# Two gate stages and two routing stages: four more row buffers, one row tile in four normalised on ScalarE, and low one-hots built on GpSimd

## The reference, cut to what matters

```python
x = _layernorm(x + attention(x))                      # layer 0; layer 1 has a wavelet part here
gate = softmax(flat_x @ w_gate.T, axis=-1)            # [4096, 8]
topk_scores, topk_idx = top_k(gate, 2)
# layer 0: out = sum over the two experts of score * expert(x)
# layer 1: counts = bincount(a_e); keep = counts <= cap (1.25 * N / E = 640)
#          pos = place of the token in its expert's queue; experts over cap give nothing
x = _layernorm(x + experts(x))
```

## Time and profile before

| what | value |
|---|---|
| median of three runs | 1922.46 us |
| profiled execution, of which span | 1918.8 us, 1917.0 us |
| gate 0, route 0 up to the first low one-hot, map of route 0 | 19.1, 20.6, 27.5 us |
| gate 1, route 1 up to the first low one-hot, map of route 1 | 19.5, 19.7, 22.8 us |
| VectorE busy in these six stretches | 13.9, 17.4, 26.9, 14.0, 16.4, 22.1 us |
| TensorE busy in them | 14.9, 0.6, 20.9, 15.6, 0.6, 17.5 us |
| ScalarE busy in them | 8.3, 1.7, 0.0, 8.4, 1.7, 0.0 us |
| GpSimd busy in them | 0.4, 1.2, 0.0, 0.5, 2.5, 0.0 us |
| granted TensorE clock in them | 0.88, 0.56, 0.89, 0.84, 0.59, 0.90 |
| share of the DMA engines in them | 0.67, 0.93, 0.49, 0.66, 0.94, 0.15 |

### The profile page before, as it was taken

How to read it: one execution, slowest core, us unless ns; L and a number is a source line. 1 busy time by engine, 2 the same in 40 slices (tenths; PEclk the granted TensorE clock), 3 DMA queues, 4 the chain that set the end, 5 groups by cost and what they waited for, 6 DMA issues and landing times. The chain is left out here.

```text
span 1917.0 us, 38671 instructions
## 1 busy us (share of the span) xinstructions
PE 1690.9 (88%) x11908; PEld 1094.2 (57%) x11909; DVE 1142.3 (60%) x2436; ACT 893.3 (47%) x1523; POOL 394.9 (21%) x559
## 2 busy tenths in 40 slices
PE   8999999999999999998489999999999399934771
PEld 4523434344434444436379999999999357923551
DVE  5688898989898999858821111111111487887224
ACT  4437777677677776771023333333333252230233
POOL 2310000000010000040023333333333100001782
PEclk9979999999999999999789999999999699977896
DMA  6501222212222221426735666665666200034545
GB/s 212 183 24 49 57 57 58 56 56 56 59 57 59 55 59 56 129 55 185 258 113 168 186 169 187 171 184 169 186 168 186 94 1 1 1 131 136 71 53 176
DMA packets 118378, 207.52 MB, mean 108 GB/s; under 512 B 22064, under 2 KB 88176, under 8 KB 108848
## 3 DMA queue, kind: packets, MB, share of 16 engines
q1 hardware_dynamic: 89280, 171.29, 28.1%
q0 software_dynamic: 20352, 22.92, 7.4%
q10 hardware_dynamic: 8688, 12.58, 1.9%
HBM read 163.65 MB, written 56.10 MB: 115 GB/s over the span
## 5 line engine op out<-in xcount | busy, mean ns | idle before, releaser
L607 DVE TENSOR_REDUCE unit_max<-ps_ring 128x1 f32<-128x512 f32 x1024 | 640.3, 684 | 76.8 <-PE ps_ring L500 70.5
L593 ACT ACTIVATE w<-ps_scores 128x1024 f32<-128x1024 f32 x512 | 498.1, 1022 | 237.5 <-PE ps_scores L562 237.4
L500 PE MATMUL ps_ring<-k_stack,q_stack 96*128 96x512 bf16 x1024 | 359.2, 392 | 10.6 <-POOL v_padded L458 7.9
L562 PE MATMUL ps_scores<-q_stack,k_stack 98*128 98x512 bf16 x1024 | 306.4, 381 | 2.6 <-ACT w L593 2.5
L1475 PEld LDWEIGHTS m_ps_h<-m_xt,w1s 128*128 128x128 f32 x2272 | 267.2, 193 | 4.6 <-issue 0.9
L1475 PE MATMUL m_ps_h<-m_xt,w1s 128*128 128x128 f32 x2272 | 267.6, 276 | 0.6 <-issue 0.6
L1485 PE MATMUL m_ps_y<-w,m_ht 128*128 x1136 | 260.8, 383 | 0.0
L522 PE MATMUL ps_o<-w,v_padded 128*32 128x256 f32 x4096 | 260.6, 383 | 0.0
L500 PEld LDWEIGHTS ps_ring<-k_stack,q_stack 96*128 96x128 bf16 x1024 | 98.6, 96 | 253.7 <-DVE unit_max L607 181.4
L1485 PEld LDWEIGHTS m_ps_y<-w,m_ht 128*128 128x128 f32 x1136 | 210.1, 190 | 29.5 <-issue 0.2
L1507 ACT ACTIVATE m_ht<-m_ps_h,w1s 128x128 f32<-128x128 f32 x568 | 162.4, 368 | 97.0 <-PE m_ps_h L1475 97.0
(11 more groups left out here) (258 smaller groups left out, 1540.9 us busy)
## 6 DMA issues: line engine op xcount, KB each, us to landing
w1s<-in_w SPq DMA_DIRECT2D x71, 1028.0 KB, 4.9
o_raw<-o_transposed SPq DMA_DIRECT2D x64, 128.0 KB
rows<-g_rows SPq DMA_DIRECT2D x16, 512.0 KB, 4.6
y<-sums SPq DMA_DIRECT2D x16, 512.0 KB, 6.5
q_parts<-qk_part SPq DMA_DIRECT2D x16, 384.0 KB, 2.8
k_parts<-qk_part SPq DMA_DIRECT2D x16, 384.0 KB, 2.8
q_stack<-q_parts SPq DMA_DIRECT2D x64, 96.0 KB
k_stack<-k_parts SPq DMA_DIRECT2D x64, 96.0 KB
```

The costliest lines, as they stand in the source:

```text
L500: nc.tensor.matmul(out[:, :], qs[0:STACK, u, qt * P:(qt + 1) * P], ks[0:STACK, u, half * HALF:(half + 1) * HALF], start=True, stop=True).t ...
L562: mm = nc.tensor.matmul(p_s[kt % 2][:, half * HALF:(half + 1) * HALF], ks[:, u, kt * P:(kt + 1) * P], qs[:, u, half * HALF:(half + 1) * HALF],
L593: nc.scalar.activation(pt[:, kt, :], p_s[kt % 2][:, :], ACT.Exp, scale=SCALE)\
L607: nc.vector.tensor_reduce(unit_max[:, u % 2, half, qt:qt + 1], src[:, :], axis=AX.X, op=ALU.max).then_inc(ring_used, count)
```

## The change

**Gates.** The row buffers become eight, so no half waits for a buffer. VectorE normalises three tiles of each half, and ScalarE the fourth (`OWN = HB - 1`), with one activation each; a new semaphore `act_ready` tells SyncE and TensorE of it. VectorE's list keeps its order.

**Routes.** The constant `unit` and the copies into `value` go: GpSimd writes the token numbers into `value` directly (two iotas), and the maxima of the softmax are written into `value` too. The mask is written as bf16 by its addition. The eight scans become one scan over 256 elements in expert-major order, whose `resets` (0 at each expert's first tile) begin it anew; totals are stored expert-major, and the order of the additions to the slot numbers changes. Slot, hi and lo are computed for both choices at once on 512 and 64 elements.

**Map.** GpSimd builds the low one-hots, one 128x128 `tensor_scalar` with `is_equal` and a scalar per partition for each product, into four buffers of a batch each. In route 1 (`tiles` is 35) the last of the eight batches stays with VectorE as one 128x1024 instruction. The loops are written out instead of being rolled.

```diff
-    HB, HALVES, BUFS, TURNS = TB // 2, 2 * B, 4, 6
+    HB, HALVES, BUFS, TURNS = TB // 2, 2 * B, 8, 6
+        act_ready = mem.sem("g_act_ready")
+        OWN = HB - 1
...
                 for h in range(HALVES):
                     sp.wait_ge(ready, h + 1)
+                    sp.wait_ge(act_ready, h + 1)
                     sp.dma_start(halves[h], st[h % BUFS][:, :, :]).then_inc(stored[h % BUFS], 16)
...
-                    for t in range(HB):
+                    for t in range(OWN):
                         last = normalised(nc, c, st[h % BUFS][:, t, :], h * HB + t)
                     last.then_inc(ready, 1)
...
+                                if k == 0 and t == OWN:
+                                    pe.wait_ge(act_ready, 2 * b + h + 1)
...
             def _(act):
+                def norm(h):
+                    wait_from(act, turned, (h - BUFS) * 2 + 2)
+                    wait_from(act, stored[h % BUFS], h // BUFS * 16)
+                    for t in range(OWN, HB):
+                        i = h * HB + t
+                        last = nc.scalar.activation(st[h % BUFS][:, t, :], c.y[:, i, :], ACT.Identity,
+                                                    scale=c.rstd[:, i:i + 1], bias=c.nmr[:, i:i + 1])
+                    last.then_inc(act_ready, 1)
...
+        LOS, LO_BUFS = 2 * NT // DEEP, 4
+        on_pool = LOS if tiles > P // 2 else LOS - 1
+
+        def low_onehots(m):
+            for k in range(2):
+                for j in range(DEEP // 2):
+                    i = m * (DEEP // 2) + j
+                    last = nc.gpsimd.tensor_scalar(oh_lo[m % LO_BUFS][:, k, j, :], iota_p[:, :], lo[:, k, i:i + 1], None,
+                                             ALU.is_equal)
+            return last
...
+                for k in range(2):
+                    nc.gpsimd.iota(value[:, k, :, 0], pattern=[[P, NT]], base=-N, channel_multiplier=1, **imprecise)\
+                        .then_inc(made, 1)
+                nc.gpsimd.memset(resets[:, :, :], 1.0).then_inc(made, 1)
...
+                pool.wait_ge(lo_ready, 1)
+                for m in range(on_pool):
+                    if m >= LO_BUFS:
+                        pool.wait_ge(mapped, (m - LO_BUFS + 1) * DEEP)
+                    low_onehots(m).then_inc(lo_made, 1)
...
-                link(v.tensor_tensor(t["mask"][:, :, :], t["oh1"][:, :, :], t["oh2"][:, :, :], ALU.add))
-                v.tensor_copy(maskb[:, :], t["mask"][:, :, :].rearrange("p i e -> p (i e)")).then_inc(mask_done, 1)
+                v.tensor_tensor(maskb[:, :].rearrange("p (i e) -> p i e", e=E), oh1, oh2, ALU.add).then_inc(mask_done, 1)
...
-                for e in range(E):
-                    scan = v.tensor_tensor_scan(out=t["incl"][:, :, e], data0=unit[:, :], data1=totals[:, :, e],
-                                                initial=0.0, op0=ALU.mult, op1=ALU.add)
-                    link(scan)
+                link(v.tensor_copy(totals[:, :, :], p_n[:, 0:G].rearrange("p (i e) -> p e i", e=E)))
+                link(v.tensor_tensor_scan(out=incl[:, :, :].rearrange("p e i -> p (e i)"),
+                                          data0=resets[:, :, :].rearrange("p e i -> p (e i)"),
+                                          data1=totals[:, :, :].rearrange("p e i -> p (e i)"),
+                                          initial=0.0, op0=ALU.mult, op1=ALU.add))
...
-                for k, onehot in enumerate((t["oh1"], t["oh2"])):
-                    link(v.tensor_tensor(t["prod"][:, :, :], t["pos"][:, :, :], onehot[:, :, :], ALU.mult))
-                    link(v.tensor_reduce(small["slot"][:, :], t["prod"][:, :, :], axis=AX.X, op=ALU.add))
...
+                link(v.tensor_tensor(prod[:, :, :, :], oh12[:, :, :, :],
+                                     bcast(t["pos"][:, :, :].unsqueeze(1), [P, 2, NT, E]), ALU.mult))
+                link(v.tensor_reduce(slot[:, :, :], prod[:, :, :, :], axis=AX.X, op=ALU.add))
...
+                v.scalar_tensor_tensor(out=lo[:, :, :], in0=hi[:, :, :], scalar=-float(P), in1=slot[:, :, :],
+                                       op0=ALU.mult, op1=ALU.add).then_inc(lo_ready, 1)
...
-                for k, gain in enumerate((small["w1"], small["w2"])):
-                    link(v.tensor_copy(value[:, k, :, 0], token[:, :]))
-                    link(v.tensor_copy(value[:, k, :, 1], gain[:, :]))
...
+                for m in range(LOS):
+                    if m >= on_pool:
+                        dve.wait_ge(mapped, (m - LO_BUFS + 1) * DEEP)
+                        shape, i0 = [P, 2, DEEP // 2, P], m * (DEEP // 2)
+                        v.tensor_tensor(oh_lo[m % LO_BUFS][:, :, :, :],
+                                        bcast(iota_p[:, :].unsqueeze(1).unsqueeze(1), shape),
+                                        bcast(lo[:, :, i0:i0 + DEEP // 2].unsqueeze(3), shape),
+                                        ALU.is_equal).then_inc(lo_last, 1)
+                    for at in range(DEEP):
+                        i, k, u = m * (DEEP // 2) + at // 2, at % 2, m % 2 * DEEP + at
+                        wait_from(dve, mapped, m * DEEP + at - 2 * DEEP + 1)
...
+                for m in range(LOS):
+                    if m < on_pool:
+                        pe.wait_ge(lo_made, m + 1)
+                    else:
+                        pe.wait_ge(lo_last, m - on_pool + 1)
```

More of the change, by code:

```diff
@@ L857, in keep @@
                         .then_inc(logits_done, 1)
+                for h in range(4):
+                    norm(h)
                 for b in range(B):
-                    norm(2 * b)
-                    norm(2 * b + 1)
+                    copy(b)
                     if b > 0:
-                        copy(b - 1)
-                    if b > 1:
-                        keep(b - 2)
-                copy(B - 1)
-                keep(B - 2)
+                        keep(b - 1)
+                    if b < 2:
+                        norm(2 * b + 4)
+                        norm(2 * b + 5)
                 keep(B - 1)
@@ L966, in stage_route @@
         ones = mem.sb("e_ones", [P, P], BF16)
-        totals = mem.sb("e_totals", [P, NT, E])
-        unit = mem.sb("e_unit", [P, NT])
+        totals = mem.sb("e_totals", [P, E, NT])
+        incl = mem.sb("e_incl", [P, E, NT])
+        resets = mem.sb("e_resets", [P, E, NT])
+        prod = mem.sb("e_prod", [P, 2, NT, E])
+        oh12 = mem.sb("e_oh", [P, 2, NT, E])
+        slot = mem.sb("e_slot", [P, 2, NT])
         iota_e = mem.sb("e_iota_e", [P, E])
@@ L985, in stage_route @@
         ownf = mem.sb("e_ownf", [P, owners])
-        oh_lo = [mem.sb(f"e_oh_lo{h}", [P, 2, DEEP // 2, P]) for h in range(2)]
+        LOS, LO_BUFS = 2 * NT // DEEP, 4
+        oh_lo = [mem.sb(f"e_oh_lo{h}", [P, 2, DEEP // 2, P]) for h in range(LO_BUFS)]
         COLS = max(P, 2 * tiles)
@@ L1065, in _ @@
                 link(v.tensor_tensor(t["pr"][:, :, :], t["ex"][:, :, :], wide(small["rc"]), ALU.mult))
-                dve.wait_ge(made, 7)
-                link(v.tensor_reduce(small["w1"][:, :], t["pr"][:, :, :], axis=AX.X, op=ALU.max))
-                first_of(t["pr"][:, :, :], small["w1"], t["oh1"])
-                link(v.scalar_tensor_tensor(out=t["pr2"][:, :, :], in0=t["oh1"][:, :, :], scalar=-2.0,
+                gains, oh1, oh2 = [value[:, k, :, 1] for k in range(2)], oh12[:, 0, :, :], oh12[:, 1, :, :]
@@ L1071, in _ @@
+                dve.wait_ge(made, 10)
+                link(v.tensor_reduce(gains[0], t["pr"][:, :, :], axis=AX.X, op=ALU.max))
+                first_of(t["pr"][:, :, :], gains[0], oh1)
+                link(v.scalar_tensor_tensor(out=t["pr2"][:, :, :], in0=oh1, scalar=-2.0,
                                             in1=t["pr"][:, :, :], op0=ALU.mult, op1=ALU.add))
-                link(v.tensor_reduce(small["w2"][:, :], t["pr2"][:, :, :], axis=AX.X, op=ALU.max))
-                first_of(t["pr2"][:, :, :], small["w2"], t["oh2"])
@@ L1087, in _ @@
+                v.tensor_tensor(totals[:, :, :], incl[:, :, :], totals[:, :, :], ALU.subtract)
+                count = incl[:, :, NT - 1]
                 if fixed is None:
@@ L1141, in outer_products @@
                         v.scalar_tensor_tensor(
                             out=oh_hi[u], in0=bcast(iota_t[:, :].unsqueeze(1), [P, 2, tiles]),
-                            scalar=hi[:, k, bass.ds(i, 1)],
-                            in1=bcast(value[:, k, bass.ds(i, 1), :].rearrange("p i a -> p (i a)").unsqueeze(2),
-                                      [P, 2, tiles]),
+                            scalar=hi[:, k, i:i + 1],
+                            in1=bcast(value[:, k, i, :].unsqueeze(2), [P, 2, tiles]),
@@ L1162, in _ @@
                     pe.wait_ge(padded, len(hi_flat))
-                def outer_products(g, first, last):
-                    for u in range(2 * DEEP):
-                        pe.wait_ge(hi_done, g * (2 * DEEP) + u + 1)
```

(12 more changed lines are left out.)

64 lines of the change are left out of this document (28 added, 36 removed).

## The result

The changed kernel is slower. Four runs gave a median of 1938.76 us (1938.31 to 1943.49), four runs of the kernel before on the same chip 1922.39 us (1920.78 to 1922.85): 1.0102 of before, 95% interval 1.0088 to 1.0116. I had forecast 1909 us, in a range of 1903 to 1922 us.

A forecast was written before the change was run, and what follows sets the result against it. VectorE was taken to lead in the gates, routes and maps, which don't overlap. Gates -2.7, routes -2.4 and -2.6, maps -4.7 and -1.0 sum to -13.4 us: 1922.5 to 1909 us; 8-in-10 range 1903 to 1922.

The forecast's parts named there:

- P: Maps: time from one GpSimd low one-hot to the next; taken as 0.30 us, with waits for VectorE 0.35 and 0.33.
- The upper bound: Maps: at a two-input addition's rate, 2.1 ns per element, plus 0.043, a GpSimd one-hot of 128 elements takes 0.46 us.
- 120 P - 54.3: Whole kernel: change in time in us with P, GpSimd's time per low one-hot, left open.
- The meetings: Maps: each VectorE high one-hot keeps GpSimd out for 0.17 or 0.09 us, adding 0.05 and 0.03 us to P.
- the fast rival: Maps: GpSimd fast and hidden, P 0.32 in route 0, TensorE bounding route 1; -19.4 us, 1903 us; chance 0.17.
- The slower rival: Maps: VectorE and GpSimd exclude each other for whole instructions, 0.58 and 0.50 us per pair; +10.8 us, 1933 us; chance 0.14.
- The routes up to lo: Routes from their start to lo, clears included: -2.4 us in route 0 and -2.6 us in route 1.
- The scan: Routes up to lo: one scan of 256 elements takes 0.70 us, replacing eight that took 2.05; -1.35 us with gaps.
- the joint slots: Routes up to lo: slot, hi and lo for both choices together take 2.44 us instead of 3.57; -1.13 us.
- The strided read: Routes up to lo: strided reads of the totals cost nothing, or 0.5 us if they ran at half rate.
- The clears: GpSimd clears five more semaphores ahead of route 0, 0.06 us each; three more before the experts' first load, 0.2 per route.
- The gates: Gate stages: -1.6 us in gate 0 and -1.1 in gate 1, in all -2.7 us (bounds -1.4 and -3.5).

The follow-up runs named there:

- the split: Changed kernel with GpSimd making only every other low batch, four of eight in route 0 and three in route 1, VectorE the others; 1909.61 us, 0.9952 of before.
- the changed kernel with the row in PSUM: Changed kernel whose high one-hots read their row of tile numbers from PSUM, copied there by ScalarE; 1938.78 us, 1.01 of before; repeated, 1937.03 us.
- the gates alone: Kernel before the change with only the new gate stage; 1919.32 us, 0.9994 of before.

## Why the prediction was wrong

- **The step that failed** is the term for P in the maps: "I take 0.30, near the copy and the select, since the one-hot reads one tensor; 0.02 is for the scalar per partition." The one-hot took 0.60 us, 0.58 from one to the next without meetings. Two parts of it were off. The difference between `tensor_scalar` and a plain cast, 0.043 us, was read on 8 elements and added to a copy of 128; it grows with the elements, and at 128 it is 0.53 - 0.29 = 0.24 us with an immediate. The scalar per partition adds 0.07, not 0.02. The upper bound had the same 0.043 on top of the two-input rate and was added up wrongly: 0.2 + 128 x 2.1 ns + 0.043 is 0.51, not 0.46. It would have been no bound at 0.51 either: I took one input to be cheaper than two, but the one-input `tensor_scalar` costs 2.6 ns per element and the two-input addition of the earlier trace rows 2.1. By the formula, 120 P - 54.3, the measured 40.11 + 34.08 us give +19.9 us; the stages of the table show +22.3.
- **The Trainium skill**, GPSIMD Engine Reference, section Elementwise — side-by-side cycle accounting, gives at best about 1.8 cycles per element. I drew an estimate of 0.41 for P from it and set it aside because of a cast in the earlier trace rows. The one-hot's 2.6 ns per element lie above the page's best case, 769 ns for 512 elements or 1.5 ns each; the cast was the wrong witness for arithmetic.
- **The meetings** were right in kind. A high one-hot of VectorE was held for up to 0.15 us by a one-hot of GpSimd (the longest took 0.52 us for the 0.37 before; 24 in 8.98 us are 0.374 each, against 0.277), the hold that the fast rival used. VectorE's batch of 1024 elements held GpSimd for 1.68 - 0.60 = 1.08 us, and 1024 x 1.04 ns are 1.07: the hold is as long as the elements stream. I had counted 0.5 for it, against my own rule. In sum the meetings moved P by 0.04 and 0.02, about as small as forecast, and that was luck in part: VectorE stood waiting for much of the map. Where it didn't, at the start of the map of route 0, five of GpSimd's one-hots took 3.36 us, 0.67 each, and in the split the high one-hots cost GpSimd 0.81 - 0.70 = 0.11 us per one-hot.
- **The slower rival** forecast 1933 us, and the time came near it by luck, by another way: the one-hots were slow alone. The rival had named one such cause, a price of the per-partition scalar, as leading "to the same place", but that scalar is 0.07 of the 0.60. Its mechanism is refuted twice, by the changed kernel with the row in PSUM and by the split. The Trainium skill, SBUF — State Buffer, section Who interferes with whom, has the later instruction blocked for the whole of the earlier one. Were that so, VectorE's 22.3 us and 32 x 0.58 on GpSimd would add up to 41 us in the split's route 0; the map took 28.45.
- **What I had taken for hidden**: TensorE's clock. At P = 0.35 a batch of products would come every 2.8 us and take 2.1 to 2.2, a wait of some 0.7 us (an estimate); at 0.627 it comes every 5.0 us. Some batches then ran at the half clock, the last of route 0 for the most part: its tail is 3.9 us against the forecast 2.6.
- **The routes up to lo** came out at -2.1 us each with the loads, for -2.4 and -2.6. The scan was right within 0.02 us; the joint slots took 2.28 us for 2.44. The strided read, which I took at nothing with 0.5 as its bound, costs 0.16, and GpSimd's constants make VectorE wait in both routes (0.42 and 0.41), where I had 0.2 in the first alone. The clears were dearer than I took them: 19 ahead of route 0 lasted 1.6 us where 14 had lasted 0.8, so five more cost 0.8 us and not 0.3. Why isn't shown; the 19 of the gates alone took 1.4 us.
- **The gates** gave -0.5 and -1.1 for -1.6 and -1.1. In gate 1 SyncE ended last, as said: its wait for the engines fell from 0.9 us to 0.2, and VectorE's at the same place rose from 0.4 to 1.0. In gate 0 it kept 1.7 us, so it was not the limit; TensorE's first 32 records took 6.49 us instead of 5.26, at the half clock for longer, while tiles were ready sooner. Before, then after, with SyncE's waits at the ends of the two gates:

```profile
898.09 5.26 PE L881 MATMUL g_ps_t<-ident,g_rows 128*128 128x128 f32 x32 [8.03 <-DVE g_rows L792]
...
900.75 6.49 PE L886 MATMUL g_ps_t<-ident,g_rows 128*128 128x128 f32 x32 [6.07 <-DVE g_rows L792]
...
SPq L824 <- PEq L824: 1.7, 1, 1.7
...
SPq L824 <- PEq L824: 0.2, 1, 0.2
```

Why the clock rose later there was not tried. In the nine other traces with the new gates, gate 0 is 17.8 to 18.9 us and gate 1 18.4 to 19.1 us, 0.4 to 1.5 and 0.6 to 1.3 us less than before, so one trace sizes neither gain.

- **The range** was also a little off its own formula, which gives 1906.6 to 1918.6 us for P from 0.32 to 0.42, not 1905 to 1917. That changes nothing here.
- **Still open** is the distance between traces (+24.7 us) and medians (+16.4). The stages that changed give +22.3 in one trace of the changed kernel and +23.4 in the other. In both measurements the recorded execution was the slowest (1943.5 and 1943.1 us). The executions that were not recorded have no trace, so what was shorter in them isn't known.
